# Summing eight expert results per token inside the expert stage of a one-core mixture-of-experts kernel, with a row ring of three batches in place of four

## The reference, cut to what matters

```python
x = x + tanh(g_ffn[1]) * L1_ffn(layernorm(x), gate_weight, gate_up_weights, down_weights)

logits = x @ gate_weight.T
routing_weights, selected_experts = top_k(softmax(logits), 8)
routing_weights = routing_weights / routing_weights.sum(-1, keepdims=True)
# for each expert e:
gu = x @ gate_up[e];  gate, up = split(gu, 2)
out = (silu(gate) * up) @ down[e]
acc = acc + combine[:, e, None] * out
```

## Time and profile before

| | us |
|---|---|
| median of the runs | 2355.81 |
| the profiled execution | 2351.87 |
| its span | 2350.1 |
| H1, from the release of stage M to the start of I1 | 1754.4 to 2240.4 |
| I1 | 2240.4 to 2350.1 |

### The profile page before, as it was taken

The page is one execution under the profiler, slowest core; times in us unless marked ns, Lnnn a source line. Parts: engine busy times, 40 slices in busy tenths (PEclk is TensorE's granted clock), DMA queues, the critical chain, the costliest instruction groups (busy, mean ns, idle before and its releaser), DMA issues. The chain is left out here.

```text
span 2350.1 us, 35817 instructions
## 1 busy us (share of the span) xinstructions
PE 1636.8 (70%) x9250; PEld 1208.8 (51%) x9250; DVE 1325.7 (56%) x3592; ACT 682.7 (29%) x1894; POOL 1045.3 (44%) x1039
## 2 busy tenths in 40 slices
PE   2959976888439999999964344441109999999800
PEld 1437754555227777777742222221108888888700
DVE  5113325656315555555536999999705555555557
ACT  1422221222013333333322222222005555555400
POOL 4031003677733333333330166666656666666600
PEclk9979986988769999999987666665559999999955
DMA  4595646533435757666314244544766666666489
GB/s 142 182 147 69 97 63 245 186 120 114 160 112 183 264 195 245 211 229 225 114 60 171 89 158 159 177 148 160 260 260 184 190 187 194 191 190 192 147 336 378
DMA packets 237104, 419.22 MB, mean 178 GB/s; under 512 B 90496, under 2 KB 170496, under 8 KB 231424
## 3 DMA queue, kind: packets, MB, share of 16 engines
q1 hardware_dynamic: 164080, 215.58, 32.3%
q0 software_dynamic: 48144, 138.57, 16.1%
q10 hardware_dynamic: 24704, 62.98, 7.7%
HBM read 253.36 MB, written 209.88 MB: 197 GB/s over the span
## 5 line engine op out<-in xcount | busy, mean ns | idle before, releaser
L896 PE MATMUL ps<-w_all,h_xT 128*128 x2112 | 546.1, 381 | 5.2 <-ACT h_xT L1119 5.2
L913 PE MATMUL ps<-w_all,h_hT 89*128 (+1 forms) x1472 | 409.7, 383 | 2.5
L640 POOL DMA_INDIRECT y_b<-h_y,h_ix x320 | 310.1, 969 | 174.9 <-issue 127.9
L623 POOL DMA_INDIRECT xs_b<-h_x,slot_of x256 | 270.9, 1058 | 244.0 <-DVE slot_of L1474 168.2
L896 PEld LDWEIGHTS ps<-w_all,h_xT 128*128 128x128 f32 x2112 | 343.3, 191 | 53.3 <-issue 9.2
L640 POOL DMA_INDIRECT y_a<-h_y,h_ix x208 | 201.7, 970 | 350.0 <-DVE h_y L1638 341.1
L889 PE MATMUL ps<-ident,h_x 128*128 128x128 f32 x1056 | 203.8, 274 | 115.3 <-DMA h_x<-xs_a 61.2
L1638 DVE TENSOR_SCALAR h_y<-ps,h_sum 128x256 f32<-128x256 f32 x528 | 254.6, 482 | 38.6 <-issue 22.8
L913 PEld LDWEIGHTS ps<-w_all,h_hT 89*128 89x128 f32 (+1 forms) x1472 | 239.2, 191 | 29.8 <-issue 6.5
L1119 ACT COPY h_xT<-ps 128x256 f32<-128x256 f32 x528 | 196.1, 371 | 151.9 <-PE ps L889 136.0
L623 POOL DMA_INDIRECT xs_a<-h_x,slot_of x192 | 190.0, 990 | 105.9 <-issue 57.9
(11 more groups left out here) (232 smaller groups left out, 2129.4 us busy)
## 6 DMA issues: line engine op xcount, KB each, us to landing
xs_b<-void_d ACTq DMA_DIRECT2D x40, 1128.0 KB, 13.1
h_x<-xs_b SPq DMA_DIRECT2D x80, 564.0 KB
c_a<-y_b SPq DMA_DIRECT2D x8, 4096.0 KB, 13.1
h_x<-xs_a SPq DMA_DIRECT2D x52, 564.0 KB, 4.2
k_a<-y_a SPq DMA_DIRECT2D x16, 1536.0 KB, 8.2
w_all<-in_exp SPq DMA_DIRECT2D x7, 2560.0 KB
qkv_d<-a_out ACTq DMA_DIRECT2D x8, 1536.0 KB, 7.4
w_all<-in_exp SPq DMA_DIRECT2D x4, 2432.0 KB
```

The costliest lines, as they stand in the source:

```text
L623: pool.indirect_dma_start(xs_d[L.name], bass.IndirectOffsetOnAxis(ap=slot_of[:, g * GT + j, k:k + 1], axis=0), h_x[:, g % NB, j, :], None) ...
L640: pool.indirect_dma_start(y_d[L.name], bass.IndirectOffsetOnAxis(ap=h_ix[:, s:s + 1], axis=0), h_y[:, s % YB, :], None).then_inc(q["y_st"] ...
L896: m = pe.matmul(ps[:, 2 + s % 2, 0:2 * L.H], h_xT[:, s % 2, c, :], w_all[:, bass.ds(e * L.W + c * 2 * L.H, 2 * L.H)], start=(c == 0), stop ...
L913: m = pe.matmul(ps[:, 6 + s % 2, 0:D], h_hT[0:w, s % 2, j, :], w_all[0:w, bass.ds(e * L.W + L.up0 + j * D, D)], start=(j == 0), stop=(j == ...
```

## The change

The ring of layer 1 has three batches (`NB_OF`), that of layer 0 keeps four. The fourth batch's place, half of a token tile's results (4 KB a partition), and a new tile `s_b` of the same size are the two `halves`; `s_x` holds two residual tiles. During H1, for the 28 tiles of tokens of the first seven groups, SP loads the two halves and the residual tile, DVE adds in four parts, spread over four consecutive tile steps at the end of each, and SP writes the finished tile out. In `sum_at` stands the step of part 0: the number of expert tiles that the groups so far can fill, 8 more, and then every 8 tiles (every 6 in the seventh group). The first are at 103, 111, 119, 127, 135; the last at 295, 301, 307, 313. SP's loop is now written out too, and at a fixed batch it calls `token_in`: at the first tile of a group it waits for all scatters of the tiles that can hold this group, otherwise for `s_done` of the tile before, then issues two loads of 512 KB, one of 128 KB, and the output of the tile before. I1 keeps the last four tiles of tokens, each with loads of 128 KB (`c_x`) and 1024 KB (`c_a`), and without `x_res`. SP's issues of H1 are behind each other in one queue, the h_x batches and the tokens' loads alike.

```diff
+SUM_ROOM = 8
+NB_OF = {"a": NB, "b": NB - 1}
...
+                s_b = s1("s_b", [P, CHOICES // 2 * D])
+                s_x = s1("s_x", [P, 2, D])
...
+        def tiles_of_groups(n):
+            return NTOK // NG * L1.K // P * n + L1.E - 1
+
+        sum_at = {}
+        for t in range(NT - GT):
+            ready = tiles_of_groups(t // GT + 1) + SUM_ROOM
+            sum_at[t] = ready + (8 if t // GT < NG - 2 else 6) * (t % GT)
+        halves = [h_x[:, NB - 1].rearrange("p j c -> p (j c)")[:, 0:CHOICES // 2 * D], s_b[:]]
+
...
-            def slots(L):
-
-                q = lay[L.name]
-                rows = xs_d[L.name].rearrange("(n p) c -> p n c", p=P)
-
-                def batch(m, s):
-                    sp.dma_start(h_x[:, s], rows[:, bass.ds(m * HB, HB), :]).then_inc(q["x_in"][s], 16)
-
-                for s in range(NB):
-                    batch(s, s)
-                n = L.tiles // HB
-
-                def next_batch(m, s):
-                    sp.wait_ge(q["t_done"], HB * (m - NB + 1) + 2)
-                    sp.wait_ge(q["ix_ready"], m - NB + 1)
-                    batch(m, s)
-
-                for b in range(1, n // NB):
-                    for s in range(NB):
-                        next_batch(NB * b + s, s)
-                for m in range(n // NB * NB, n):
-                    next_batch(m, m % NB)
-
             def of_tokens(L):
                 return y_d[L.name][0:NTOK * CHOICES, :].rearrange("(g t p k) d -> g p t (k d)", g=NG, p=P, k=CHOICES)
 
-            def sums(L):
+            out_v = out.rearrange("(t p) d -> t p d", p=P)
+
+            def token_in(t):
+                if t % GT == 0:
+                    n = tiles_of_groups(t // GT + 1)
+                    for s in range(YB):
+                        sp.wait_ge(lay["b"]["y_st"][s], 16 * ((n - s + YB - 1) // YB))
+                if t:
+                    sp.wait_ge(s_done, t)
+                of = of_tokens(L1)[t // GT, :, t % GT, :]
+                for h in range(2):
+                    sp.dma_start(halves[h], of[:, h * CHOICES // 2 * D:(h + 1) * CHOICES // 2 * D]).then_inc(s_in[h], 16)
+                if t >= 2:
+                    sp.wait_ge(out_st, 16 * (t - 1))
+                sp.dma_start(s_x[:, t % 2], x_d[:, t * D:(t + 1) * D]).then_inc(sx_in, 16)
+                if t:
+                    token_out(t - 1)
+
+            def token_out(t):
+                sp.dma_start(out_v[t], s_x[:, t % 2]).then_inc(out_st, 16)
+
+            def slots(L):
 
                 q = lay[L.name]
-                src = of_tokens(L)
-                with sp.Fori(0, NG // 2) as b:
-                    for s in range(2):
-                        g = 2 * b + s
-                        sp.wait_ge(q["a_used"], g + 1)
-                        if L is L1:
-                            sp.dma_start(x_res[:, bass.ds(g * GT, GT), :].rearrange("p t d -> p (t d)"),
-                                         x_d[:, bass.ds(g * GT * D, GT * D)]).then_inc(q["a_in"][s], 16)
-                        sp.dma_start(c_a[:, s, :, 0:L.K * D],
-                                     src[bass.ds(g, 1), :, :, 0:L.K * D].rearrange("o p t d -> (o p) t d"))\
-                          .then_inc(q["a_in"][s], 16)
-
+                nb = NB_OF[L.name]
+                rows = xs_d[L.name].rearrange("(n p) c -> p n c", p=P)
+                load_at = {}
+                if L is L1:
+                    for t, step in sum_at.items():
+                        load_at.setdefault((step - SUM_ROOM + 3) // HB + nb - 1, []).append(t)
+                n = L.tiles // HB
+                for m in range(max(n, max(load_at, default=0) + 1)):
+                    if m < n:
+                        if m >= nb:
+                            sp.wait_ge(q["t_done"], HB * (m - nb + 1) + 2)
+                            sp.wait_ge(q["ix_ready"], m - nb + 1)
+                        sp.dma_start(h_x[:, m % nb], rows[:, m * HB:(m + 1) * HB, :]).then_inc(q["x_in"][m % nb], 16)
+                    for t in load_at.get(m, []):
+                        token_in(t)
...
+            sp.wait_ge(s_done, NT - GT)
+            token_out(NT - GT - 1)
+            for j in range(GT):
+                t = NT - GT + j
+                sp.dma_start(c_x[:, j], x_d[:, t * D:(t + 1) * D]).then_inc(c_in[j], 16)
+                sp.dma_start(c_a[:, j], of_tokens(L1)[NG - 1, :, j, :]).then_inc(c_in[j], 16)
+            for j in range(GT):
+                sp.wait_ge(c_done, j + 1)
+                sp.dma_start(out_v[NT - GT + j], c_x[:, j]).then_inc(out_st, 16)
+            sp.wait_ge(out_st, 16 * NT)
...
+                adds_at = {}
+                for t, step in sum_at.items():
+                    for part in range(4):
+                        adds_at.setdefault(step + part, []).append((t, part))
+
+                def add_token(t, part):
+
+                    gate = tgate[:, 3:4]
+                    x_t = s_x[:, t % 2, :]
+                    if part < 2:
+                        a = halves[part]
+                        dve.wait_ge(s_in[part], 16 * t + 16)
+                        dve.tensor_tensor(a[:, 0:2 * D], a[:, 0:2 * D], a[:, 2 * D:4 * D], ALU.add)
+                    elif part == 2:
+                        dve.drain()
+                        dve.tensor_tensor(halves[0][:, 0:2 * D], halves[0][:, 0:2 * D], halves[1][:, 0:2 * D], ALU.add)
+                        dve.drain()
+                        dve.tensor_tensor(halves[0][:, 0:D], halves[0][:, 0:D], halves[0][:, D:2 * D], ALU.add)
+                    else:
+                        dve.wait_ge(sx_in, 16 * t + 16)
+                        dve.drain()
+                        dve.scalar_tensor_tensor(x_t, halves[0][:, 0:D], gate, x_t, ALU.mult, ALU.add)\
+                           .then_inc(s_done, 1)
...
+                        if L is L1:
+                            for t, part in adds_at.get(j, []):
+                                add_token(t, part)
...
-            sums(L1, tgate[:, 3:4])
+            for j in range(GT):
+                dve.wait_ge(c_in[j], 32)
+                dve.tensor_tensor(c_a[:, j, 0:4 * D], c_a[:, j, 0:4 * D], c_a[:, j, 4 * D:8 * D], ALU.add)
+                dve.drain()
+                dve.tensor_tensor(c_a[:, j, 0:2 * D], c_a[:, j, 0:2 * D], c_a[:, j, 2 * D:4 * D], ALU.add)
+                dve.drain()
+                dve.tensor_tensor(c_a[:, j, 0:D], c_a[:, j, 0:D], c_a[:, j, D:2 * D], ALU.add)
+                dve.drain()
+                dve.scalar_tensor_tensor(c_x[:, j], c_a[:, j, 0:D], tgate[:, 3:4], c_x[:, j], ALU.mult, ALU.add)\
+                   .then_inc(c_done, 1)
```

More of the change, by code:

```diff
@@ L236, in flamingo @@
             s_ = sb_in(st)
-            c_a = s_("c_a", [P, 2, GT, CHOICES * D])
+            s_("h_x", [P, NB, HB, RW])
+            c_a = s_("c_a", [P, GT, CHOICES * D])
+            c_x = s_("c_x", [P, GT, D])
             assert nc.sbuf_base <= nc.sbuf_top - big
@@ L317, in flamingo @@
                 y_st=[sem(f"y_st{n}{s}") for s in range(YB)],
-                a_in=[sem(f"a_in{n}{s}") for s in range(2)],
-                a_used=sem(f"a_used{n}"),
-            )
+            )
+        s_in = [sem(f"s_in{h}") for h in range(2)]
+        sx_in = sem("sx_in")
+        s_done = sem("s_done")
+        c_in = [sem(f"c_in{j}") for j in range(GT)]
+        c_done = sem("c_done")
         wk_y = sem("wk_y")
@@ L468, in weights1, with of_tokens @@
                     e0 = e1
+            def of_tokens(L):
+                return y_d[L.name][0:NTOK * CHOICES, :].rearrange("(g t p k) d -> g p t (k d)", g=NG, p=P, k=CHOICES)
+            out_v = out.rearrange("(t p) d -> t p d", p=P)
[14 more added lines that the diff above has]
+                    token_out(t - 1)
@@ L885, in tr @@
                 def tr(i, s, b):
+                    nb = NB_OF[L.name]
                     if s % HB == 0:
-                        pe.wait_ge(q["x_in"][s // HB], 16 * b + 16)
+                        pe.wait_ge(q["x_in"][i // HB % nb], 16 * (i // HB // nb) + 16)
                     for c in range(KC):
-                        m = pe.transpose(ps[:, s % 2, c * P:(c + 1) * P], h_x[:, s // HB, s % HB, c * P:(c + 1) * P],
-                                         ident[:])
+                        m = pe.transpose(ps[:, s % 2, c * P:(c + 1) * P],
+                                         h_x[:, i // HB % nb, s % HB, c * P:(c + 1) * P], ident[:])
                     m.then_inc(q["t_done"], 1)
@@ L1221, in _ @@
                 dve.sem_inc(lay[L.name]["y_done"], YB)
-                dve.sem_inc(lay[L.name]["a_used"], 2)
             def group_stats(g):
@@ L1599, in experts, with compare, pick @@
                 q = lay[L.name]
-                def compare(i, m, b):
-                    dve.wait_ge(q["x_in"][m], 16 * b + 16)
-                    dve.tensor_tensor(h_oh[:, :, 0:CHOICES], h_x[:, m, :, D:D + CHOICES],
+                nb = NB_OF[L.name]
+                def compare(i):
+                    slot = i // HB % nb
```

(41 more changed lines are left out.)

2 lines of the change are left out of this document (removed).

## The result

The changed kernel took 2301.01 us (median of 4, 2299.31 to 2303.15) where the kernel before took 2356.07 beside it: a ratio of 0.9762, 95% interval 0.9746 to 0.9777. A second comparison on another occasion gave 0.9763 (0.9747 to 0.978). The forecast was 2291 in a range of 2271 to 2326.

What follows compares the result with a forecast made beforehand. The prediction took H1 to be bound by PE and I1 by bytes. Its terms, -87.5 for I1, +19 for additions and +4 for the last group, sum to -64.5: 2355.8 becomes 2291 us, range 2271 to 2326.

Steps and rivals of the forecast that it cites:

- I1: Last stage: shrinks from 109.66 us to four tokens' worth, 22.2 us, a gain of 87.5 us (83 to 90).
- DVE's additions: In H1: four parts a token overrun PE's spare 0.39 us by 0.68 us, 28 times, 19 us (0 to 36).
- DMA in H1, regular tokens: In H1: the added 116 GB/s, 302 in all, passes and regular tokens' loads land in time, costing nothing.
- waits of DVE for DMA only at the last three tokens: Sign expected in H1's profile: DVE waits for loads at no token but the last three.
- The first token of a group waits for y_st ... in time as well: In H1: a group's first load goes at 99.5 steps for step 103, after the scatter lands, so in time.
- The last group: End of H1, tokens six steps apart: loads land late, 1.2 us each for three tokens, 4 us (0 to 9).
- The ring of three: H1's h_x batches: three instead of four still arrive with 3 us of room, charged 0 (0 to 4 us).
- D: Rival, H1: the ring of three runs dry, PE waits for batches, kernel slower than before, up to 2375 us; chance 0.03.
- What would show it: Signs listed: last stage 20 to 27 us with 16 DVE instructions, H1 longer by 19 to 27 us.
- A: Rival, H1: the additions are absorbed, H1 keeps its length but for 4 us, 2272 us; chance 0.11.
- B: Rival, H1: loads land late on busy DMA engines, DVE waits every time, 42 us, 2333 us; chance 0.15.
- C: Rival, H1: DVE's additions wait for POOL's scatters, 1.3 us a token, 37 us, 2328 us; chance 0.06.

Runs made afterwards that it cites:

- x2b: The change with seven eighths of the bytes of the 28 tokens' result loads left out, all additions kept: 2291.68 us, H1 488.1 us.
- x5: The change with additions in five parts, both halves freed a step before the gated sum, next h_x batch issued ahead of the output: 2288.34 us, ratio 0.971.
- x8: x5 with room of 12 tiles instead of 8, loads one h_x batch later, 27 tokens instead of 28, all 8 steps apart: 2275.55 us, ratio 0.9664.
- x1b: The change without the additions of the 28 tokens in H1; loads, waits and outputs stay: 2278.59 us, H1 479.7 us.
- x3: The change with a ring of four batches, an own place for the first half, weights of only 32 experts loaded: 2292.99 us, H1 493.7 against 498.1.
- x7b: The change with all additions three steps later, the places of SP's waits unchanged: 2395.5 us, H1 593.2 us.
- x4b: The change with the additions in five steps instead of four: 2302.93 us, ratio 0.9781, H1 496.8 us.

## Why the prediction was right, and where it was off

- **I1**: 22.2 us and a gain of 87.5 were worked out; 21.0 and 88.7 came. The first data were expected at 6.0 and came at 6.2; a token took 2.96 us instead of 3.2, as the next token's first add starts before the last instruction of this one ends (the fourth came 3.28 us after the third, as its bytes were late); the tail was 2.5 instead of 3.4.
- **DVE's additions** (19 us): the mechanism is shown, in the timeline of a token (0.67 us of PE's waits, 0.68 worked out) and by x2b, in which they alone remain: 21.9 us for 24 tokens, 0.91 each, and 25.3 in all. This is the term that was off most, 6 us: a third too small. The working counted PE's idle time only, 0.68 us. In x2b the starts of L1657 lie 2.19, 1.81, 0.65 and 1.81 us apart over a token's steps, 6.46 in place of 5.67 us, so a token costs 0.8 us. Every second token costs 0.97 us (12.88 against 11.91 for its eight steps): its part 1 falls into the first step of a new `body` of 16 tiles, a step that took 1.9 us before the change too. Why the additions cost more just there was not found.
- **DMA in H1, regular tokens** (0): here a step of the argument failed, and with it the sign "waits of DVE for DMA only at the last three tokens". "The first token of a group waits for y_st ... in time as well" did not hold. In the change these loads left 4.2 to 5.6 us ahead of their use rather than the 5.6 of the working, and a load of 512 KB took 4.7 us (median) rather than the 3.7 of the earlier trace rows; at tokens 4 and 16 that was too late. For token 4:

```profile
1956.88 0.33 SPq L502 DMA_DIRECT2D h_x<-y_b  x1
...
1962.18 0.69 DVE L1680 TENSOR_TENSOR h_x<-h_x 128x512 f32<-128x512 f32 x1 [1.00 <-DMA h_x<-y_b]
```

  These waits are 2.7 us in the change; 27.1 less the additions' 21.9 leaves 5.2 for all that the DMAs did to regular tokens. For the other regular tokens the working held: loads left 5.8 us or more ahead (5.5 worked out) and none was late. x5, in which the first tokens from 4 on had 3.8 to 4.7 us, shows the waits at just these tokens, and x8, which gives them 5.5 or more, has 0.7 us of them in all.
- **The last group** (4 us): 8.4 us stood there. Additions alone gave 2.6 (x2b) and loads alone 2.8 (x1b); the other 3 arise where both meet.
- **The ring of three** (0): 4.4 us, by x3. The working had such a batch land 8 us after s_done with "3 us of room"; in x7b it landed 10 us after. In the change PE waited for batches by 3.3 us in all, behind the loads of tokens 4 and 8: the sign named for D, on a small scale.
- **Forecast against the sum**: +23 for H1 and +35.3 measured, which is outside the 19 to 27 that "What would show it" gives H1. The time is in range since the gain of I1, by far the largest term, was right within 1.2 us, and since the range left room for 35 us above the forecast. The median came out 10 us above it, inside the likeliest case's own range of 2280 to 2305.
- **Rivals**: A (absorbed) is out by x2b. B (busy engines make loads late everywhere) is out by x8, which moves more bytes a second with 0.7 us of such waits; late loads at certain tokens were part of the truth. C (DVE waits for POOL) is out: adds of 684 to 694 ns, while POOL's scatter rose from 969 to 989 ns in the mean. The timeline shows which side pays:

```profile
2238.18 0.97 POOL L663 DMA_INDIRECT y_b<-h_y,h_ix  x1 [0.45 <-issue]
2238.85 0.69 DVE L1680 TENSOR_TENSOR h_x<-h_x 128x512 f32<-128x512 f32 x1 [1.46 <-DMA h_x<-y_b]
...
2240.58 0.69 DVE L1680 TENSOR_TENSOR s_b<-s_b 128x512 f32<-128x512 f32 x1 [0.39 <-DMA s_b<-y_b]
...
2240.89 1.23 POOL L663 DMA_INDIRECT y_b<-h_y,h_ix  x1 [1.74 <-DVE h_y L1664]
```

  Of the change's scatters in H1 the 36 that start while an add of 512 runs last 1.14 us in the mean, the 39 during which such an add starts 0.97, as long as the rest; the 43 adds that start while a scatter runs last 0.68 us, as long as the rest. By the rule of the Trainium skill, page "SBUF — State Buffer", section "Who interferes with whom", that the second one to start blocks fully, these 43 adds should have stood too; this trace agrees on POOL's side only, as stage M did.
  D (slower, the queue dry) did not happen in the change, but x7b shows that it was three steps away: same mechanism, 2395.5 us.

## What to carry to other kernels

Work moved beside a saturated engine costs what it overruns that engine's slack at each step, so spread it: five parts instead of four took a token from 0.78 to 0.17 us where no load was late (x4b). And when the overrun is taken away, look at once for the load that was covered by it (x4b: nothing gained until x5 and x8 also moved the loads). Give every load the same distance between the moment it may be issued and the moment it is used, and count what stands behind a waiting instruction on the queue of DMAs: here three steps decided between 2301 and 2395 us.

## What the runs showed that I had not expected

- The kernel before took 2356 to 2358 us on two chips and 2571 on a third (7 runs, 2555.3 to 2577.78). In the variants that were profiled there the first 96 tiles of H1 took 166 to 169 us instead of 139, at a granted clock of 0.99, with waits that the profile puts down to "issue". There the additions and the loads each cost nothing that the measure shows. The cause stays open.
- At 293 GB/s and a DMA share of 0.88 (x8) a load of 512 KB still landed in 4.7 us (median), as in the change at 275 GB/s; 3.7 for such a load in the kernel before.
